# Index tables and node statistics in one block, and graph layers whose carry goes through a closing matmul

## The reference, cut to what matters

```
def _L0_gnn_ref(x, src, dst, gamma, beta, W, b):
    ones = jnp.ones(src.shape[0], dtype=x.dtype)
    out_deg = jnp.clip(jax.ops.segment_sum(ones, src, num_segments=N), 1.0)
    in_deg = jnp.clip(jax.ops.segment_sum(ones, dst, num_segments=N), 1.0)
    src_norm = (out_deg ** (-0.5))[:, None]
    dst_norm = (in_deg ** (-0.5))[:, None]
    for i in range(n_layers):
        mu = jnp.mean(x, axis=0)
        var = jnp.var(x, axis=0)
        x = (x - mu) * jax.lax.rsqrt(var + EPS) * gamma[i] + beta[i]
        h = x * src_norm
        agg = jax.ops.segment_sum(h[src], dst, num_segments=N) * dst_norm
        x = jax.nn.relu(agg @ W[i] + b[i])
    return x
...
x = x + _L0_gnn_ref(_layernorm(x, axis=-1), src, dst, ...)
```

## Time and profile before

| | |
|---|---|
| time, median of 3 runs | 4214.27 us (4212.77 to 4214.78) |
| time of the profiled execution | 4210.74 us |
| its span in the trace | 4209.0 us |
| busy over the span, PE / DVE / ACT / POOL | 81% / 63% / 29% / 34% |
| stages 1 to 5 in the trace | 6.2 to 1144.1 us |
| the stages behind them, untouched | 1144.1 to 4209.0 us |

### The profile page before, as it was taken

The page is one execution under the profiler, slowest core; times in us unless marked ns, Lnnn a source line. Parts: engine busy times, 40 slices in busy tenths (PEclk is TensorE's granted clock), DMA queues, the critical chain, the costliest instruction groups (busy, mean ns, idle before and its releaser), DMA issues. The chain is left out here.

```text
span 4209.0 us, 60863 instructions
## 1 busy us (share of the span) xinstructions
PE 3413.8 (81%) x16811; PEld 2667.0 (63%) x16812; DVE 2659.6 (63%) x6025; ACT 1239.1 (29%) x2287; POOL 1414.7 (34%) x1753
## 2 busy tenths in 40 slices
PE   4876377888877410899999999999949996688999
PEld 3610255666677410788888888888838884575766
DVE  7765797894367677454544545445428887776776
ACT  0122144452211100443443434344311111113443
POOL 0176387783255201132222222223113330006552
PEclk9999699999955555899999999999979998798999
DMA  1043222333399401454544534445322210126664
GB/s 51 0 126 80 63 93 83 110 97 120 118 310 310 150 0 36 131 143 102 144 124 113 134 102 137 128 107 142 95 71 60 58 55 17 74 94 147 160 156 107
DMA packets 254792, 457.41 MB, mean 109 GB/s; under 512 B 66065, under 2 KB 71482, under 8 KB 254064
## 3 DMA queue, kind: packets, MB, share of 16 engines
q1 hardware_dynamic: 180899, 288.95, 20.9%
q0 software_dynamic: 62368, 145.38, 15.8%
q10 hardware_dynamic: 11318, 20.54, 1.3%
HBM read 327.73 MB, written 126.85 MB: 108 GB/s over the span
## 5 line engine op out<-in xcount | busy, mean ns | idle before, releaser
L1336 PE MATMUL experts_psU<-experts_x_hi,experts_up_hi 128*128 128x312 f32 (+1 forms) x1408 | 436.8, 310 | 15.4 <-issue 11.8
L1337 PE MATMUL experts_psU<-experts_x_lo,experts_up_hi 128*128 128x312 f32 (+1 forms) x1408 | 436.6, 310 | 0.0
L1338 PE MATMUL experts_psU<-experts_x_hi,experts_up_lo 128*128 128x312 f32 (+1 forms) x1408 | 435.9, 310 | 0.0
L1350 PE MATMUL experts_psO<-experts_dn_hi,experts_hid_hi 128*104 128x512 f32 (+1 forms) x1056 | 421.5, 399 | 0.0
L1351 PE MATMUL experts_psO<-experts_dn_lo,experts_hid_hi 128*104 128x512 f32 (+1 forms) x1056 | 415.4, 393 | 0.0
L1352 PE MATMUL experts_psO<-experts_dn_hi,experts_hid_lo 128*104 128x512 f32 (+1 forms) x1056 | 415.4, 393 | 0.0
L1296 POOL DMA_INDIRECT experts_xg<-xn,experts_token_i x96 | 100.6, 1048 | 768.6 <-DVE experts_token_i L1432 749.1
L1464 DVE TENSOR_TENSOR experts_hid_lo<-experts_hid,experts_hid_hi 128x312 fp32r<-128x312 f32 (+1 forms) x352 | 161.6, 482 | 231.5 <-ACT experts_hid L1398 228.2
L1456 DVE TENSOR_TENSOR experts_dn_lo<-experts_dn_raw,experts_dn_hi 128x1536 fp32r<-128x1536 f32 (+1 forms) x128 | 207.9, 1624 | 122.5 <-ACT experts_dn_hi L1384 122.5
L1336 PEld LDWEIGHTS experts_psU<-experts_x_hi,experts_up_hi 128*128 128x128 f32 (+1 forms) x1408 | 265.4, 188 | 19.3 <-issue 17.3
L1396 ACT ACTIVATE experts_hid_hi<-experts_psU,experts_bup 128x312 fp32r<-128x312 f32 (+1 forms) x352 | 183.7, 522 | 296.7 <-PE experts_psU L1338 260.3
(11 more groups left out here) (391 smaller groups left out, 8506.9 us busy)
## 6 DMA issues: line engine op xcount, KB each, us to landing
experts_dn_raw<-in_L_ffn_W_down SPq DMA_DIRECT2D x96, 768.0 KB, 4.6
experts_up_raw<-in_L_ffn_W_up SPq DMA_DIRECT2D x32, 682.5 KB, 10.0
conv<-gcn_diff SPq DMA_DIRECT2D x80, 256.0 KB, 2.0
stats_xt<-in_x SPq DMA_DIRECT2D x78, 256.0 KB, 2.7
route_xt<-in_x SPq DMA_DIRECT2D x78, 256.0 KB, 4.8
x<-route_xt SPq DMA_DIRECT2D x78, 256.0 KB, 4.3
xn<-route_xn ACTq DMA_DIRECT2D x78, 256.0 KB, 4.8
two_xt<-x SPq DMA_DIRECT2D x78, 256.0 KB, 2.8
```

The lines of the kernel that those rows point to most:

```text
L1336: pe.matmul(acc, up_hi[:, c, cols], x_hi[:, c, :], start=(c == 0), stop=False)
L1337: pe.matmul(acc, up_hi[:, c, cols], x_lo[:, c, :], start=False, stop=False)
L1338: mm = pe.matmul(acc, up_lo[:, c, cols], x_hi[:, c, :], start=False, stop=(c == C - 1))
L1350: pe.matmul(psO[0:S, q, :], hid_hi[0:w, m, s], dn_hi[0:w, m, :], start=(m == 0), stop=False)
```

## The change

`index_tables` and `records_and_stats` become one block, `index_and_stats`. The tables are transposed: the low part (128) lies on the partitions, the high part (80) along the row. The high one-hots per row (`hirow`, `is_hi_row`, L297 and L298) go; instead PE turns the low one-hots tile by tile (`turn`), and ACT copies them out as `pick`. The first 40 node tiles are normalized beside the histograms, the other 39 beside the lookups. The normalization itself goes from DVE to ACT, which takes a shift that POOL computes. Records of four edge tiles at a time get their degrees' root (`grade`), and are scattered without a staging copy, four tiles behind the lookup.

```diff
-            tiles(pe, ET, [(0, histogram)])
...
-            tiles(pe, ET, [(0, lookup)])
+            for t in range(ET):
+                if t >= 2:
+                    pe.wait_ge(counted, t - 1)
+                for n in range(2):
+                    mm = pe.matmul(psH[:, t % 2, n * NH:(n + 1) * NH], is_lo[:, n, t, :], is_hi[:, n, t, :],
+                                   start=True, stop=True)
+                mm.then_inc(histed, 1)
+                add_up(t)
...
+            for t in range(ET):
+                j = t % 2
+                if t + 1 < ET:
+                    turn(t + 1)
+                if ET + t < NT:
+                    add_up(ET + t)
+                pe.wait_ge(picked, t + 1)
...
+                pe.matmul(psL[:, j, 0:3 * NH], pick[:, j, 0, :], tab[:, 0:3, :].rearrange("l c h -> l (c h)"),
+                          start=True, stop=False)
...
+            for t in range(ET):
+                act.wait_ge(turned, t + 1)
+                if t >= 2:
+                    act.wait_ge(looked, t - 1)
+                act.copy(pick[:, t % 2, :, :].rearrange("l n p -> l (n p)"), psT[:, t % 2, 0:2 * P]).then_inc(picked, 1)
+                if ET + t < NT:
+                    norm_and_square(ET + t)
...
+            for t in range(ET):
+                j = t % 2
+                if ET + t < NT:
+                    stats(ET + t)
+                takes.at(t)
...
+                v.wait_ge(looked, t + 1)
+                takes.go(v.tensor_tensor(prod[:, 0:3, :], psL[:, j, 0:3 * NH].rearrange("p (c h) -> p c h", h=NH),
+                                         is_hi[:, 0, t, :].unsqueeze(1).to_broadcast([P, 3, NH]), ALU.mult))
```

```diff
-            step(v.tensor_tensor_scan(wsum[:, ::-1], same[:, ::-1], wrow[:, ::-1], 0.0, ALU.mult, ALU.add))
-            step(v.tensor_tensor(g.link[:, 0:ET - 1, :], key[:, 0:ET - 1, :],
-                                 key[:, 1:ET, 0:1].to_broadcast([P, ET - 1, P]), ALU.is_equal))
+            v.tensor_tensor(link[:, :].rearrange("o (t l) -> o t l", l=P), key[0:1, 0:ET, :],
+                            key[0:1, 1:ET + 1, 0:1].to_broadcast([1, ET, P]), ALU.is_equal).then_inc(linked, 1)
...
+            for k in range(ET // G):
+                pe.wait_ge(weighed, (k + 1) * G)
+                if k >= 2:
+                    pe.wait_ge(low, k - 1)
+                pe.matmul(psW[0:1, k % 2, :], g.ones[:, 0:1],
```

```diff
-                for h in range(C):
-                    of = zero[:, 0:1] if isinstance(s, int) and s == 0 else agg[:, (j - 1) % R, h, 0:1]
-                    v.scalar_tensor_tensor(agg[:, j, h, :], g.link[:, tile(s), :], of, psA[:, j, h * P:(h + 1) * P],
-                                           ALU.mult, ALU.add).then_inc(carried, 1)
...
+            def close(s, j):
+                at_least(pe, wstaged, s, 0)
+                at_least(pe, carried, s, 1)
...
                 pe.matmul(psZ[:, j % 2, :], ws[:, j, :], vb[:, :], start=False, stop=True).then_inc(projected, 1)
...
+            def carry(s, j):
                 at_least(act, projected, s, 0)
...
+                act.copy(vb[0:1, :], psZ[0:1, j % 2, :]).then_inc(carry_high, 1)
...
+            def lower_carry(s, j):
+                at_least(v, carry_high, s, 0)
+                v.tensor_tensor(vb[32:33, :], psZ[0:1, j % 2, :], vb[0:1, :].bitcast(F32), ALU.subtract)\
+                    .then_inc(carried, 1)
```

More of the change, by code:

```diff
@@ L251, in _, with add_up @@
+            grade(ET // G - 1)
+            for t in range(ET - G, ET):
+                scatter(t)
+            pool.wait_ge(scattered, 16 * 2 * ET)
         @block.tensor
         def _(pe):
+            def add_up(n):
+                r, k = node_rows(g, n), n % G
+                pe.wait_ge(normed, n + 1)
+                pe.matmul(psN[0:1, :], g.ones[0:r, 0:1], xn[0:r, k, :], start=(n == 0), stop=(n == NT - 1))
+                pe.wait_ge(squared, n + 1)
+                mm = pe.matmul(psQ[0:1, :], g.ones[0:r, 0:1], xsq[0:r, k, :], start=(n == 0), stop=(n == NT - 1))
+                mm.then_inc(all_summed if n == NT - 1 else summed, 1)
@@ L253, in _, with turn @@
+            def turn(t):
+                if t >= 2:
+                    pe.wait_ge(picked, t - 1)
+                for n in range(2):
+                    mm = pe.matmul(psT[:, t % 2, n * P:(n + 1) * P], is_lo[:, n, t, :], identb[:, :], start=True, stop=True)
+                mm.then_inc(turned, 1)
             pe.wait_ge(hot, 1)
-            def histogram(t, j):
-                at_least(pe, counted, t, 2)
+            for t in range(ET):
+                if t >= 2:
+                    pe.wait_ge(counted, t - 1)
@@ L346, in take @@
-                chain.end()
-            tiles(v, ET, [(0, take)])
-            v.wait_ge(look_step, 5 * ET)
-            for n in range(2):
-                step(v.scalar_tensor_tensor(place_f[:, n, :], look[:, :, 2 + 2 * n], 1.0, earlier[:, :, n],
-                                            ALU.add, ALU.add))
-            step(v.tensor_copy(place[:, :, :], place_f[:, :, :]))
-            for n in range(2):
-                step(v.tensor_scalar(deg[:, n, :], look[:, :, 1 + 2 * n], 1.0, None, ALU.max))
@@ L389, in gcn_tables @@
-        wsum = ph.sb("wsum", [1, EP])
+        key = ph.sb("key", [P, ET + 1, P])
+        link = ph.sb("link", [1, EP], F32R)
+        unlink = ph.sb("unlink", [1, EP], F32R)
         parts = ph.sb("parts", [1, 2, EP], F32R)
-        turned = ph.sb("turned", [ET, 2, P])
+        turned = ph.sb("turned", [ET, P])
         psT = ph.ps("psT", [P, 512])
-        loaded, transposed, copied, stored, rows, step_done, one, scanned, high, split, placed = (
-            ph.sem(n) for n in ("loaded", "transposed", "copied", "stored", "rows", "step", "one", "scanned", "high",
-                                "split", "placed"))
+        psW = ph.ps("psW", [P, 2, 512])
@@ L396, in gcn_tables @@
+        loaded, transposed, copied, stored, rows, step_done, one, linked, unlinked, weighed, summed, high, low, placed = (
+            ph.sem(n) for n in ("loaded", "transposed", "copied", "stored", "rows", "step", "one", "linked", "unlinked",
+                                "weighed", "summed", "high", "low", "placed"))
         block = ph.block()
@@ L753, in sq_diff @@
                     .then_inc(squared, 1)
-            tiles(act, ET, ([] if last else [(6, sq_diff)]) + [(4, rectify), (1, heighten), (0, stage_w)], R)
+            tiles(act, ET, [(L + 4, carry)] + ([(1, norm)] if first else []) + [(L + 1, heighten), (L + 1, stage_w)]
+                  + ([] if last else [(L + 5, sq_diff)]), R)
         @block.vector
```

680 lines of the change are left out of this document (339 added, 341 removed).

## The result

The changed kernel takes 4299.99 us (median of 3, 4295.84 to 4307.11) against 4214.27 us: a ratio of 1.0214, with a 95% interval of 1.0200 to 1.0229. The forecast of 4304 us lies 4 us beside it. Stages by windows, columns as in the earlier trace rows: the whole index block, its first loop (histograms), its second loop (lookups), the layer tables, and layers 0, 1 and 2.

The account below looks back on a forecast made before the run. No engine was taken to bound all the changed stages. Index and statistics +169, tables -9, layer 0 -44, layer 1 -23 and layer 2 -3 gave +90 us on 4214.3, so 4304 us; range over all 4205 to 4345.

Parts of the forecast that it names:

- The ring of the lookups: Lookup loop: statistics, sums, lookup and products run one after another, tile by tile; 10.3 us a turn, 402 us.
- The sum of the index block: Index and statistics: 28 + 118 + 7 + 402 + 22, ending at 577 us instead of 408.2: +169 us.
- The clock: Lookup loop: TensorE at the low clock after its pauses, 10.4 us a turn instead of 7.8.
- The first loop: Histograms beside 40 node tiles: two tiles pass in 5.0 + 0.7 us, 2.9 a tile, 116 us.
- The tables: Layer tables: 55 us against 64.4, mainly the scan's 10.81 us: -9 us.
- Layer 1 and 2: Layer 1 at PE's pace of 4.28 us a tile, -23 us; layer 2 with a shorter start, -3 us.
- Layer 0: Layer 0: 4.3 to 4.5 us a tile, 216 us against 260.8: -44 us.
- (a): Lookup loop: the ring at the high clock, 7.8 to 8.3 us a tile, kernel 4205 to 4230 us; chance 0.13.
- (b): Lookup loop: tiles overlap and POOL bounds, about 4.6 us a tile, kernel 4082 us; chance 0.08.
- (c): Lookup loop: POOL's power held up by DVE's two `same`, +0.55 us a turn, kernel 4325 us; chance 0.10.
- (d): Layers: carry chain longer than its 3.6 us of cover; at 4.4 us, 96 us more, kernel 4400 us; chance 0.05.
- (e): Layers 0 and 1: adds on DVE delay PE as POOL did, 67 us missing, kernel 4371 us; chance 0.06.

Follow-up runs that it names:

- e1: Changed kernel with PE's sums of node tile 40+t put behind lookup t instead of ahead of it; 4086.81 us.
- e2: Changed kernel with DVE taking the statistics of node tile 41+t, one further ahead, before it waits for lookup t; 4111.47 us.
- e4: Changed kernel with 16 unread bf16 matmuls put ahead of each node tile's sums in the lookup loop; 4226.43 us.
- e9: e3 with the node tiles' sums beside the histograms issued two tiles late; 4036.63 us, in a second run 4031.61 us.
- e5: e3 with the layers' adds into total and square moved back from DVE to POOL; 4100.48 us.
- e8: Kernel before the change with only the adds into total and square moved from POOL to DVE; 4160.19 us.
- e7: e9 without the carry: ACT's copy and DVE's subtraction left out, the closing matmul not waiting for them; 4022.38 us.
- e10: e9 with one of layer 0's two adds (total) on POOL, the other on DVE; 4030.23 us.
- e3: Changed kernel with both order changes, that of e1 on PE and that of e2 on DVE; 4065.11 us.
- e11: e9 with unread half-row copies ahead of ACT's copy of the carry, 2 in layer 1 and 8 in layer 2; 4037.06 us.

## Why the prediction was right, point by point

- **The ring of the lookups.** Shown by e1 and e2, each of which opens it at one joint, and by the circle of waits. Its terms: to the shift's end 2.55 us (forecast 2.34: the power takes 0.66 instead of 0.57, and the way to it 1.42 instead of 1.29), ACT 0.81, sums 3.50 (3.40), lookup to products 2.05 (2.12), products and reduction 1.24 (1.26). Forecast 10.3, measured 10.26 in the mean of the 38 turns. The clock came back within some lookups: a pass of L372 takes from 0.37 to 0.77 us, with a median of 0.61.
- **The sum of the index block, in part by luck.** 577 forecast, 576.5 measured, but the terms were off and cancel. I charged 39 turns, 402 us, and had overlooked that the last step holds no node tile: 392.1. The scans and tables took 11.0 where 7 were priced, the first loop 119.5 where 118, and from the last lookup to the end of the stage it was 25.9 where 22. In the whole kernel, too, layer 0's 8 us too much are made up by the tables (3.5), layer 1 (2.6) and layer 2 (1.0).
- **The clock.** Taken from a pause in another stage: the granted clock of the loop was 0.66. e4 prices it at some 2.1 us a turn, where I had 2.6 between the ends. PE paused 4.53 us ahead of psN in the turn shown, 4.8 in the mean. The Trainium skill ("TensorE: Matmul & The Clock Gate", section "HAM oscillation — how this bites in real kernels") says that short bursts between waits begin at the low clock again; the trace agrees, with 1.7 us for each sum where 0.85 is the price at the high level.
- **The first loop.** Forecast 2.9 a tile, measured 2.98. e9 shows its ring by opening it.
- **The tables.** Forecast -9, measured -12.5: the adjacency took 10.3 us (600.53 to 610.84) where 13 were priced, since its 40 instructions of 0.33 overlap, and the key landed 18.6 us into the stage instead of 19.5; the tail of group sums took 12.8 where 12 were priced, and the weights' transfers hid.
- **Layer 1 and 2.** -23 and -3 forecast, -25.6 and -4.0 measured, but the reason for layer 1 was half of the truth. "Layer 1 went slower since `agg_lo` took 3.38 us": e5 and e8 showed that POOL's pace was the bound, 4.51 us a tile of its own and 4.95 beside the blocked `agg_lo`: the long `agg_lo` entered through POOL's index copy, not through DVE. The size came out right since both readings end at TensorE's 4.28, which is luck as far as the mechanism goes.
- **Layer 0.** -44 forecast, -36.1 measured: the term "4.3 to 4.5 us a tile" was too small by 0.4. I had summed DVE's instructions at 0.6 each (they take 0.69), and hadn't looked for a ring there, although I had just found one in the index block. e7 and e10 showed that DVE's sum doesn't matter.
- **The rivals.** (a) wasn't the case, but e4 is nearly it, made by force: mostly 7.80 a turn, 8.28 in the mean, and 4226 us. (b) is what e3 makes of the kernel: with no ring, POOL is the bound at 4.37 us, and 4065 us against the 4082 worked out. (c) was worth 0.1 us a turn and not 0.55: the power took 0.66 beside the two `same`. (d) and (e) fell by e7, e11 and the layers' times.

## What to carry to other kernels

When two loops are merged, write down for each engine what stands ahead of what, and follow one tile through all engines: if the way ends at an instruction that stands ahead of the next tile's first one, the tiles run one by one, however little each engine has to do. Issue a consumer's late work behind the next producer's early work; here that cost no instruction and gave 5.7 us a step in the mean of 39. In a profile, look for engines that are each half idle and whose releasers point round in a circle; and doubt an engine whose busy time fills the tile until something taken off it shortens the tile.

## What the runs showed of the hardware

- Filling a pause of TensorE with 16 matmuls that nobody reads saved some 70 us (e4), as the following fp32 sums fell from 1.7 to 0.85 us each in three turns of four.
- A POOL copy of one column took 0.65 us beside a DVE subtraction that POOL was holding up, and 0.18 where that subtraction read one operand from PSUM (before and e5, layer 1).
- In the lookup loop of the kernel before, PE worked without a pause for over 100 us (110.00 of the 110.00 us from 80 to 190), with the durations of 1.2 GHz (896 columns in 3.00 us), while the profile's clock column read 1.00. In e1 and e3, with the tables on 128 partitions instead of 80, a median pass of L370 took 0.42 us for 240 columns where one of L272 had taken 0.85 for 384, and the two ends of L370 in e1 are 0.37 and 0.71. What made the passes long before stays open.
